# Both self attentions in the padded fp32 form, and one stream of the last attention started eight steps late

## The reference, cut to what matters

```python
# L1_attn: rotary tables on q and k
scores = jnp.einsum('bhsd,bhtd->bhst', q, k) * SCALE
attn = jax.nn.softmax(scores, axis=-1)
out = jnp.einsum('bhst,bhtd->bhsd', attn, v)
# L1_ffn: the last attention, one mask over keys for "pos" and one for the others
pos = sim > 0.9
x_pos = masked_attn(pos)
x_neg = masked_attn(~pos)
reg_out = (x_pos[:, :REG] + x_neg[:, :REG]) * 0.5
tok_out = jnp.where(pos[:, :, None, None], x_pos[:, REG:], x_neg[:, REG:])
```

## Time and profile before

| | us |
|---|---|
| median of 3 runs | 2320.46 (2318.49 to 2326.34) |
| the profiled execution's own time | 2325.29 |
| its span | 2323.5 |
| first self attention section of each round (4 rounds) | 101, 95, 94, 94 |
| last attention, from its first transposes to the last layer norm | about 415 |
| one middle round of it | 105.5 |

### The profile page before, as it was taken

One profiled execution on the slowest core, in us unless ns is written; L12 is line 12 of the kernel. 1 busy time (PEld: TensorE's weight loads), 2 busy tenths in 40 slices (PEclk: granted clock), 3 DMA queues, 4 the chain that ended last, 5 costly groups with the idle time before them and its releaser, 6 DMA issues.

```text
span 2323.5 us, 30395 instructions
## 1 busy us (share of the span) xinstructions
PE 1759.7 (76%) x12736; PEld 1506.3 (65%) x12736; DVE 1172.5 (50%) x2262; ACT 918.3 (40%) x1115; POOL 431.9 (19%) x375
## 2 busy tenths in 40 slices
PE   6685886858799999995686688668767837666666
PEld 6575775656688888884575576557556736555555
DVE  3354443554353333336743754384256436768577
ACT  2443423334322333222641643363236334553735
POOL 1210200102223444432023012302211130000000
PEclk9887888878889999997598676758776866665655
DMA  4000000000300000000000000000000010000000
GB/s 169 1 1 0 1 1 1 1 0 1 163 15 14 28 28 21 8 1 1 1 1 28 1 1 0 28 1 1 28 0 1 1 65 17 28 24 23 1 10 10
DMA packets 8631, 42.14 MB, mean 18 GB/s; under 512 B 1072, under 2 KB 3376, under 8 KB 7472
## 3 DMA queue, kind: packets, MB, share of 16 engines
q1 hardware_dynamic: 8496, 40.21, 4.6%
HBM read 31.82 MB, written 8.39 MB: 17 GB/s over the span
## 4 chain that ended last, share of the span: by engine, by line
PE 56%; DVE 27%; ACT 10%; POOL 3%; issue 3%; DMA 1%; SPq 0%; POOLq 0%; DVEq 0%; ACTq 0%
PE ps L93 12%; PE ps L94 11%; PE ps L95 11%; DVE m L1327 10%; PE ps L544 7%; DVE sm L1338 5%; ACT r L1006 4%; DVE m L1338 4%; PE ps L662 4%; PE ps L606 2%; PE ps L612 2%; DVE m L1335 2%; ACT m L1006 2%; POOL sm L1909 2%; DVE r L1327 1%
## 5 line engine op out<-in xcount | busy, mean ns | idle before, releaser
L544 PE MATMUL ps<-cst,m 128*128 128x128 f32 (+2 forms) x1408 | 249.8, 347 | 150.6 <-POOL m L1823 53.3
L1006 ACT ACTIVATE r<-ps 128x512 fp32r<-128x512 f32 (+2 forms) x232 | 167.2, 748 | 457.4 <-PE ps L544 432.0
L544 PEld LDWEIGHTS ps<-cst,m 128*128 128x128 f32 (+2 forms) x1408 | 215.0, 189 | 191.3 <-POOL m L1823 58.1
L1006 ACT ACTIVATE m<-ps 64x308 f32<-64x308 f32 (+5 forms) x240 | 172.8, 727 | 389.9 <-PE ps L95 227.0
L1327 DVE TENSOR_TENSOR m<-m 128x1024 f16<-128x1024 f32 (+4 forms) x248 | 217.7, 910 | 59.3 <-ACT m L1006 32.7
L1793 POOL TENSOR_SCALAR sm<-sm 128x2 f32<-128x2 f32 x40 | 10.1, 252 | 1163.2 <-DVE sm L1354 1163.2
L1327 DVE TENSOR_TENSOR r<-ps,r 128x512 fp32r<-128x512 f32 x120 | 82.1, 690 | 276.0 <-ACT r L1006 275.8
L1327 DVE TENSOR_TENSOR m<-m,ps 128x1024 f32<-128x1024 f32 (+1 forms) x64 | 71.7, 1120 | 265.7 <-PE ps L95 189.1
L1338 DVE TENSOR_REDUCE sm<-ps 128x68 f32<-128x204 f32 (+2 forms) x208 | 114.9, 555 | 119.6 <-PE ps L646 96.6
L1338 DVE TENSOR_REDUCE m<-ps 128x4 f32<-128x1024 f32 (+1 forms) x144 | 155.0, 1140 | 23.3 <-PE ps L805 20.5
L93 PE MATMUL ps<-r,w0h 128*128 128x256 f32 x448 | 135.1, 302 | 38.7 <-DVE r L1327 38.4
(11 more groups left out here) (183 smaller groups left out, 4434.4 us busy)
## 6 DMA issues: line engine op xcount, KB each, us to landing
raw<-wu_dram SPq DMA_DIRECT2D x12, 768.0 KB, 4.0
keep_dram<-m SPq DMA_DIRECT2D x8, 768.0 KB, 3.3
m<-keep_dram SPq DMA_DIRECT2D x8, 768.0 KB, 4.3
w1raw<-w_dram SPq DMA_DIRECT2D x1, 3840.0 KB, 14.5
w0raw<-w_dram SPq DMA_DIRECT2D x3, 1024.0 KB, 19.0
w1f<-w1f_dram SPq DMA_DIRECT2D x1, 2048.0 KB, 18.9
out_dram<-xres SPq DMA_DIRECT2D x16, 128.0 KB, 1.8
xres<-x_dram SPq DMA_DIRECT2D x1, 1536.0 KB, 12.9
```

What stands on the lines that cost most here:

```text
L544: return pe.transpose(o, i, ident[0:n, 0:n])
L1006: return act.activation(o, i, ACT.Copy)
```

## The change

`a1` and `fa` get another form of the attention, shared by both. A head takes 32 columns instead of 64 (16 of value, one for the maximum, two for the mask, the rest zeros), all in plain fp32 and without parts; so four heads are transposed at once (`turn_heads`) and each sits in a group of 32 rows. The scores for the maxima are 32 products of 32 rows a batch, four at a time in different row groups and banks (`maxima_of`), with one reduction of 128x2048 for four heads. `attend` has eight units of two heads: four fp32 products of 32 rows, one exponential, and for every second unit eight fp32 products with 32-column values in four column groups. The sum of the weights comes from a column of ones in the values. The result is copied (`out_of`), transposed back (`turn_out`), divided (`divide`) and projected as before, in bank 2 instead of bank 0. The registers' products take the same form (`xt`, `xm`, `x2`, `xs`, `xo`). The copies `st0`, `st1`, `vh`, `vm`, and the subtractions `tl`, `vr`, `vl`, `pl` go. In `fa` the layout of the next batch is done by DVE alone, and every engine's queue of stream 1 begins `LAG` = 8 steps after that of stream 0; a batch has 22 steps on each engine.

The new code, cut to its core:

```diff
+LAG = 8
...
             for b in batches:
-                nxt = b + 2 if b + 2 < B else None
-                f = {"pe": F_PE, "act": F_ACT, "dve": F_DVE}[eng]
+                nxt = [(b + 2, s) for s in FFRONT] if b + 2 < B else [None] * 6
                 if b < 2:
-                    o += [(b, s) for r in f for s in r]
-                m = {"pe": M_PE, "act": M_ACT, "dve": M_DVE}[eng]
-                rm = {"pe": [["rt"], ["rx0"], ["rx1"], []], "act": [["bd"], [], [], []], "dve": [[], ["nx0"], ["nx1"], ["dg"]]}[eng]
-                o += [(b, s) for s in turns([*m, rm], (0, 0, 0))]
-                w = [r[("pe", "act", "dve").index(eng)] for r in W_R]
-                rg = {"pe": [["rs"], ["ro"]], "act": [["re"], []], "dve": [["rl"], ["r3", "rr", "ox"]]}[eng]
...
+        def attn_views(v, st, m, r, p, o):
+            v.QK = m[:, 0:2048].rearrange("p (j h n) -> p j h n", j=2, h=32)
+            v.qT, v.kT = (m[:, a:a + 1024].rearrange("p (c n) -> p c n", c=4) for a in (2048, 3072))
+            v.P = [m[:, a:a + 1024] for a in (p, p + 1024, p + 2048)]
+            v.OT = m[:, o:o + 1024].rearrange("p (c n) -> p c n", c=4)
+            v.o = k2(m[:, o + 1024:o + 1536])
+            v.oT = tuple(k2(r[:, 512 * i:512 * (i + 1)]) for i in range(2))
+            v.rc = st.sm[:, 64:96].rearrange("p (j h) -> p j h", j=2)
...
+            def turn_heads(st, o, v, h0, step):
                 for c in range(4):
                     for j in range(2):
-                        m = tp(pair(st, i)[:, c * 256 + j * 128:c * 256 + (j + 1) * 128], s[:, j, 2 * c:2 * c + 2, :].rearrange("p h n -> p (h n)"))
+                        m = tp(o[:, c * 256 + j * 128:c * 256 + (j + 1) * 128], v.QK[:, j, h0 + 4 * c:h0 + 4 * c + 4, :].rearrange("p h n -> p (h n)"))
...
+            def maxima_of(st, b, v, sig, dve_):
+                for c in range(4):
+                    if c:
+                        pe.wait_ge(*dve_.at(b, f"nm{c - 1}"))
+                    for j in range(2):
+                        for a in range(4):
+                            r = 32 * a
+                            m = pe.matmul(bank(st, a)[:, 256 * j:256 * j + 256], v.qT[r:r + 32, c, 128 * j:128 * j + 128], v.kT[r:r + 32, c, :], start=True, stop=True)
+                    m.then_inc(sig.up(b, f"mx{c}"), 1)
+                    yield
+                pe.wait_ge(*dve_.at(b, "nm3"))
+
+            def attend(st, b, v, sig, act_, dve_, first):
+                def weigh_values(c):
+                    pe.wait_ge(*act_.at(b, f"e{2 * c + 1}"))
+                    if c > 1:
+                        pe.wait_ge(*dve_.at(b, f"ot{c - 2}"))
+                    for k in range(2):
+                        for a in range(4):
+                            w = v.P[(2 * c + a // 2) % 3].rearrange("p (a k n) -> p a k n", a=2, k=2)
+                            m = pe.matmul(bank(st, 2 + c % 2)[32 * a:32 * a + 32, 0:256], v.va[:, k, 4 * c + a, :], w[:, a % 2, k, :], start=k == 0, stop=k == 1)
+                    m.then_inc(sig.up(b, f"o{c}"), 1)
+
+                for u in range(8):
+                    pe.wait_ge(*(act_.at(b, f"e{u - 1}") if u else first))
+                    for k in range(2):
+                        for a in range(2):
+                            r = 64 * (u % 2) + 32 * a
+                            m = pe.matmul(bank(st, a)[:, 256 * k:256 * k + 256], v.kT[r:r + 32, u // 2, 128 * k:128 * k + 128], v.qT[r:r + 32, u // 2, :], start=True, stop=True)
+                    m.then_inc(sig.up(b, f"s{u}"), 1)
+                    if u and u % 2 == 0:
+                        weigh_values(u // 2 - 1)
+                    yield
+                weigh_values(3)
+
+            def turn_out(st, b, v, sig):
+                for c in range(4):
+                    for j in range(2):
+                        m = tp(bank(st, j)[:, 128 * c:128 * c + 128], v.OT[:, c, 128 * j:128 * j + 128])
+                m.then_inc(sig.up(b, "t3"), 1)
+
+            def project_out(st, b, v, w, sig, dve_):
                 for c in range(2):
                     for j in range(2):
-                        m = tp(bank(st, 0)[:, c * 256 + j * 128:c * 256 + (j + 1) * 128], v.o[:, j, c * 128:(c + 1) * 128])
+                        m = tp(bank(st, 2)[:, c * 256 + j * 128:c * 256 + (j + 1) * 128], v.o[:, j, c * 128:(c + 1) * 128])
                 m.then_inc(sig.up(b, "oT"), 1)
                 yield
                 pe.wait_ge(*dve_.at(b, "oT"))
@@ -869,27 +793,27 @@
...
-                if nxt is not None:
-                    work_.append(front(st, nxt))
-                yield from beside(work_)
-                yield
-                for i in range(2):
-                    pe.wait_ge(*dve_.at(b, f"on{i}3"))
+                pe.wait_ge(*st.f_pool.at("clean"))
+                pe.wait_ge(*dve_.at(b, "f"))
+                turn_heads(st, pair(st, 0), v, 16, sig.up(b, "tk"))
+                turn_heads(st, pair(st, 1), v, 0, sig.up(b, "tq"))
+                yield
+                pe.wait_ge(*act_.at(b, "Tk"))
+                pe.wait_ge(*dve_.at(b, "xq"))
+                for c in range(4):
+                    m = tp(bank(st, 0)[:, 32 * c:32 * c + 8], v.qs[:, 4 * c:4 * c + 4, :].rearrange("p h n -> p (h n)"), 8)
+                m.then_inc(sig.up(b, "xt"), 1)
+                yield
+                pe.wait_ge(*act_.at(b, "xe"))
+                for c in range(4):
+                    for a in range(4):
+                        r = 32 * a
+                        m = pe.matmul(bank(st, a)[32 * c:32 * c + 32, 0:256], v.qx[r:r + 32, c, :], v.kT[r:r + 32, c, :], start=True, stop=True)
+                m.then_inc(sig.up(b, "xm"), 1)
+                yield
+                pe.wait_ge(*dve_.at(b, "nx"))
+                yield from maxima_of(st, b, v, sig, dve_)
+                turn_heads(st, pair(st, 1), v, 0, sig.up(b, "t2"))
+                tp(bank(st, 0)[:, 0:128], v.nx.rearrange("p c n -> p (c n)")).then_inc(sig.up(b, "x2"), 1)
+                yield
+                pe.wait_ge(*act_.at(b, "T2"))
+                pe.wait_ge(*dve_.at(b, "x2"))
+                for k in range(2):
+                    for c in range(4):
+                        for a in range(4):
+                            r = 32 * a
+                            m = pe.matmul(bank(st, a)[:, 32 * k + 8 * c:32 * k + 8 * c + 8], v.kT[r:r + 32, c, 128 * k:128 * k + 128], v.qx2[r:r + 32, c, 0:8], start=True, stop=True)
+                m.then_inc(sig.up(b, "xs"), 1)
+                yield
+                yield from attend(st, b, v, sig, act_, dve_, act_.at(b, "ex"))
+                pe.wait_ge(*act_.at(b, "e7"))
+                for c in range(4):
+                    for k in range(2):
+                        for a in range(4):
+                            m = pe.matmul(bank(st, 0)[32 * a:32 * a + 32, 8 * c:8 * c + 8], v.va[:, k, 4 * c + a, :], v.px[:, a, 32 * k + 8 * c:32 * k + 8 * c + 8], start=k == 0, stop=k == 1)
+                m.then_inc(sig.up(b, "xo"), 1)
+                yield
+                pe.wait_ge(*dve_.at(b, "xo"))
...
+            def attend(st, b, v, sig, pe_):
+                for u in range(8):
+                    act.wait_ge(*pe_.at(b, f"s{u}"))
+                    if u > 2:
+                        act.wait_ge(*pe_.at(b, f"o{(u - 3) // 2}"))
+                    act.activation(v.P[u % 3], pair(st, 0), ACT.Exp, scale=0.25).then_inc(sig.up(b, f"e{u}"), 1)
+                    yield
+
...
-            for st in streams:
...
+            def maxima_of(st, b, v, sig, pe_):
+                for c in range(4):
+                    dve.wait_ge(*pe_.at(b, f"mx{c}"))
+                    reduce(v.QK[:, :, 4 * c:4 * c + 4, 16].rearrange("p j a -> p a j"), st.ps[:, :].rearrange("p (a j n) -> p a j n", a=4, j=2),
+                           ALU.max, negate=True).then_inc(sig.up(b, f"nm{c}"), 1)
+                    yield
+
+            def out_of(st, b, v, sig, pe_, c):
+                dve.wait_ge(*pe_.at(b, f"o{c}"))
+                dve.tensor_copy(v.OT[:, c, :], bank(st, 2 + c % 2)[:, 0:256]).then_inc(sig.up(b, f"ot{c}"), 1)
+
+            def divide(st, b, v, sig, pe_):
+                dve.wait_ge(*pe_.at(b, "t3"))
+                src = pair(st, 0).rearrange("p (j h n) -> p j h n", j=2, h=16)
+                dve.reciprocal(v.rc, src[:, :, :, 16]).then_inc(sig.up(b, "rc"), 1)
+                dve.wait_ge(*sig.at(b, "rc"))
+                tt(v.o.rearrange("p j (h n) -> p j h n", h=16), src[:, :, :, 0:16], v.rc.unsqueeze(3).to_broadcast([P, 2, 16, 16]), ALU.mult).then_inc(sig.up(b, "on"), 1)
+
...
+                        out_of(st, b, v, sig, pe_, u // 2 - 1)
+                    yield
+                out_of(st, b, v, sig, pe_, 3)
+                dve.wait_ge(*pe_.at(b, "xo"))
+                dve.tensor_copy(v.ox_[:, :, 0:8], bank(st, 0)[:, 0:32].rearrange("p (c n) -> p c n", c=4)).then_inc(sig.up(b, "xo"), 1)
+                yield
+                divide(st, b, v, sig, pe_)
...
```

(5 more changed lines are left out.)

605 lines of the change are left out of this document (155 added, 450 removed).

## The result

Four runs of the changed kernel gave 2196.8 us in the median (2178.6 to 2203.6), four of the kernel before 2323.4: a ratio of 0.9442, 95% interval 0.9374 to 0.9511. The forecast was 2304 us, inside whose range (2195 to 2385) the result just falls; the direction was right, the size eight times too small. Direction and range owe something to luck: the prediction itself gave "faster" no more than 0.51, and the result lies 2 us inside the edge. The profiled execution took 2190.1 us (span 2188.0), 135 less than that of before.

A forecast was written before the change was run, and what follows sets the result against it. It took ACT to bound weighing and DVE the maxima, with PE's clock low. Self attentions -19, last attention +5 and earlier first transposes -2 made -16 us on 2325.3, 4.8 above the median: 2304 us, range 2195 to 2385.

The forecast's parts named there:

- rival 3: Narrow fp32 products don't run side by side on PE, in both attention stages: 2455 us, chance 0.06.
- rival 2: PE at 1.2 GHz becomes the bound: +3 us in the self attentions, +45 in the last, 2365 us; chance 0.25.
- the forecast's 0.85: Maxima: a group of eight fp32 products takes 0.85 us at 2.4 GHz, assuming full overlap of four row groups.
- So I keep the present share of 28% at 2.4 GHz: Attention stages: 28% of time stays at 2.4 GHz, giving -19 us for four self attention rounds.
- the forecast's own table: Self attention round -19 us at 2.4 GHz, +0.8 at 1.2; last attention round 76 or 110 us.
- The row it rested on: Cross attention: the same work ran at clock 0.97 one round, 0.50 for 20 us the next, PE busy throughout.
- Rival 1: Clock stays up in most attention stretches: 2150 us throughout, 2200 with two thirds of it; chance 0.15.
- some us either way: Cross attention and fq: unchanged work takes 12 or 20 us by clock, so each round may move some us.
- surcharge of +5: Last attention: four offset rounds plus start and end take 420 us against 415, so +5.
- rival 4: Last attention: the offset couples the streams badly, pairs 15% longer, +60 us, 2364 us; chance 0.06.

The follow-up runs named there:

- e9: Changed kernel with both streams of the last attention in step, and eight unread transposes behind each of attend's first two scores, both self attentions: 2220.7 us, ratio 0.9541.
- e17: e9 with twelve more unread transposes in one piece behind each stream's small register products, ahead of attend in the last attention: 2165.5 us, ratio 0.9246.
- e5: Changed kernel with three unused ScalarE copies ahead of the third turn's copy of each stream in a1, so attend begins later: 2232.8 us, ratio 0.9583.
- e3: Changed kernel with LAG 0, both streams of the last attention in step: 2190.7 us, ratio 0.9409.
- e4: Kernel before with the second stream of the last attention begun eight steps behind, nothing else changed: 2362.1 us, ratio 1.0141.
- e14: e9 with 60 of the 64 small register products left out for each stream and round of the last attention: 2153.4 us, ratio 0.9205.
- e13: e3 with 60 of the 64 small register products left out for each stream and round of the last attention: 2174.6 us, ratio 0.9323.
- e7: Changed kernel, offset kept, with eight unread transposes behind each of attend's first two scores, both streams and both self attentions: 2157.1 us, ratio 0.9246.
- e8: e7 with two more unread transposes ahead of each group of four small register products in the last attention: 2220.7 us, ratio 0.9529.
- e15: Changed kernel, offset kept, with four unread transposes behind each of attend's first two scores in a1 and eight in the last attention: 2191.1 us, ratio 0.9379.
- e12: Kernel before with four unread transposes ahead of each block of value products in its two self attentions: 2358.9 us, ratio 1.0147.

## Why the prediction was right and wrong

**Right: the mechanism and the prices at either clock.** ACT stops being the bound of `attend` (busy for 17.1 of 27 us at 1.00); two units take 10.95 and 6.39 us against 11.15 and 6.4; the row groups run side by side in plain fp32 (rival 3 fell: eight products of maxima, 16 records, within 1.15 us at 2.4 GHz, where one after the other 3.4 were due, an estimate from the 0.43 us of a record with twice the columns in the earlier trace rows); a reduction of 128x2048 takes 2.2 us back to back against the 2.3 chosen; PE at 1.2 GHz is the bound, busy for 39.80 of 41 us, and round 0's `attend` is what rival 2 describes. The 3.4 us reckoned for one after the other became 1.15 with the tail counted, a factor of 3.0, where the forecast's 0.85 took it as four. The difference cost nothing in the maxima, where DVE is the bound: five reductions back to back in 11.09 us.

**Wrong: "So I keep the present share of 28% at 2.4 GHz".** That step failed. In `a1` the mean clock was 0.69 in round 0 and 0.89 to 0.92 after it, a share of about 0.38 and 0.8; in the last attention 0.76, a share of 0.52. Put into the forecast's own table these shares give -52 us for `a1` in place of -19, and rounds of 92 us, -30 in place of +3, for the last attention: 66 of the 119 us that were missing. The row it rested on (dense PE at 0.50 for 20 us) was read as "work doesn't bring the clock back, so the share stays". The first half holds in e9 and in e17's first round (54 and 58 us at 0.50 with PE busy throughout), though not always: in e5's rounds 1 and 3 the clock came back. The second doesn't follow: a clock that isn't lost needn't come back, and the share was measured on another kernel, whose TensorE waited for ACT. In `a1`, and in the last attention in step (e3), `attend` ran nearly always at one level from about its first score to its end, so a round there had two answers, and the forecast's mean was neither. With the offset of eight the clock changed within `attend`, and the round of 85.5 us lies between the table's 76 and 110. Rival 1, given 0.15, was what happened in three of `a1`'s four rounds; that the total came out near its 2200 is in part luck, since the clock in the last attention stayed far below it.

**Two sizes.** Rounds 1 to 3 of `a1` saved 22.6 to 24.1 us, more than the 19 priced for 2.4 GHz throughout, and round 0 saved 8.7 where its share gives 6.7; the part ahead of the first exponential is 12 to 15 us shorter (forecast 9 to 11), the part behind it 10 (forecast 7.8) or 6 longer (forecast 9.7): 26 us in the four rounds. The last attention's table was 6.5 us a round too long at the measured clock (92 against 85.5), 15 us in all with its ends. The cross attention's -15 was named as "some us either way" and not counted. These 66, 26, 15 and 15 us, less the 3 lost ahead of `a1`, are the 119. How much of the 26 is the clock too, in the parts around `attend`, isn't separated. Small slips changed nothing: rival 2's own terms, +3 and +45, make 2368 and not 2365, its turning point lies by the forecast's table at about a fifth of the time at 2.4 GHz and not a sixth, and 16 weight loads in 1.95 us are 0.122 us each and not 0.112.

**The offset** was priced at nothing much and is nothing (e3); its surcharge of +5 was within what can be told. On the old form it costs 32 us (e4), about half of what rival 4 priced for the new one.

**What stays open:** what tips the clock at the entry. e14's two rounds have the same 9 us of instructions ahead of `attend` and differ in what lies before. In e13's and e17's first rounds it fell about the third turns, whose two blocks stand 1 us apart, and in e13's others just behind the first score. Filling TensorE went with a kept clock in more rounds (`attend` at 0.86 to 0.97 in e7, at 0.98 to 1.00 in three rounds of e17), filling it in small pieces with a lost one (0.58 in that stretch of e8). e15 against e7, which differ only in `a1`'s transposes (four behind a score in place of eight), shows that a setting isn't a guarantee; the two ran on different chips, and no run tells whether that matters. Each count of rounds here is from one profiled execution.

## What to carry to other kernels

Where a stage makes TensorE the bound, cost it at both levels of the clock and give each answer a chance; the mean clock of the old kernel isn't a number to scale with, since it can be a mixture of two levels (the 0.64 of the earlier trace rows holds the 0.50 of the earlier trace rows and 1.00 from 1087 to 1097 us), and a stage may run at one of them from its first products to its end (0.51 for 40 us in e3, 1.00 for 27 us in `a1`'s rounds 1 to 3). Look at what stands ahead of the stage: where turns stood with 1 us of waiting between them, `attend` in step had the upper level in none (e9, e13), two (e14) or three (e17) of four rounds. There it is worth trying a block of dense work in one piece, useless if need be: 3.1 us of it a round took `attend` from 53 us to 30 in three of four rounds (e17 against e9), and e7 and e17 are 2% faster than the change with all their extra work. But relieve the other engines first: on the old form ScalarE was busy for 32.66 of 33 us, and filling TensorE made it slower (e12, ratio 1.0147).

## What the runs showed of the hardware

- `attend` ran at 0.51 in one round and at 1.00 in the next, behind the same 9 us of TensorE instructions with starts equal to 0.01 us (e14), and 58 us of unbroken work at 0.50 didn't raise the clock (e17), while in e5's round 1 it rose after 10 us in which TensorE was busy for 7.3.
- Small blocks of transposes (2) between groups of small products (8 records) cost more than the same work in one piece: e8's groups took 0.70 us a pair at 2.4 GHz (1941.10 to 1941.81), where e17 has 0.24 us for eight records of products and 0.24 for two transposes (64 records and 12 transposes, each in one piece, 1951.40 to 1954.75).
- Plain fp32 products on four row groups of 32 overlap: 16 records of 256 columns in 1.15 us at 2.4 GHz and in 1.9 to 2.1 at 1.2 (the changed kernel, L742).
